# Windowed attention on one core: scores and values of each head in one matmul, own-window scores only, and another column order in the gather

## The reference, cut to what matters

```python
# 16 clouds of 512 points; 4 sorted orders; each point sees 10 neighbours per order
neigh = gather(feats, inds)                                 # per order: [B, N, 10, C], C = 32
gf = jnp.concatenate([broadcast(center), neigh - center], axis=-1)
x = stack(4 orders)[..., perm].reshape(B * N, 10, 8 * C)    # 8 heads of 32
x16 = x.astype(float16)
qh = x16.reshape(B * N, 10, nheads, 32)
scores = einsum('bihd,bjhd->bhij', qh, qh) / sqrt(32)
attn = softmax(scores, axis=-1)                             # over the 10 neighbours j
out = einsum('bhij,bjhd->bihd', attn, qh)
fused = out @ W_lin.T + b_lin                               # then conv, instance norm, leaky relu, max
```

## Time and profile before

| | before |
|---|---|
| median of 3 runs | 2311.37 us (2306.75 to 2311.55) |
| span of the profiled execution | 2306.2 us |
| DVE, PE, ACT, POOL busy in the span | 1904.0, 1865.0, 1616.7, 1007.8 us |
| SP and ACT queues' share of 16 DMA engines | 39.2% and 0.8% |

### The profile page before, as it was taken

How to read it: one execution, slowest core, us unless ns; L and a number is a source line. 1 busy time by engine, 2 the same in 40 slices (tenths; PEclk the granted TensorE clock), 3 DMA queues, 4 the chain that set the end, 5 groups by cost and what they waited for, 6 DMA issues and landing times. The chain is left out here.

```text
span 2306.2 us, 99850 instructions
## 1 busy us (share of the span) xinstructions
PE 1865.0 (81%) x37528; PEld 1286.8 (56%) x37528; DVE 1904.0 (83%) x3658; ACT 1616.7 (70%) x3249; POOL 1007.8 (44%) x995
## 2 busy tenths in 40 slices
PE   0296665888888566499999998677999999999967
PEld 0023335777777344389999997343554544454432
DVE  6798986999999599689989987783888888888865
ACT  0299985888888699689999998456555555555532
POOL 0000006999999200178888886001434444444311
PEclk9997668999999666699999999799999999999979
DMA  2103766666565167655555552212322322222210
GB/s 59 14 1 89 165 163 141 123 122 123 122 123 121 32 157 166 157 110 109 107 105 110 108 105 53 93 28 67 92 83 73 91 74 81 79 85 82 61 56 19
DMA packets 435513, 216.09 MB, mean 94 GB/s; under 512 B 301259, under 2 KB 404843, under 8 KB 435304
## 3 DMA queue, kind: packets, MB, share of 16 engines
q1 hardware_dynamic: 430120, 210.73, 39.2%
q10 hardware_dynamic: 5312, 4.31, 0.8%
HBM read 161.97 MB, written 52.96 MB: 93 GB/s over the span
## 5 line engine op out<-in xcount | busy, mean ns | idle before, releaser
L865 PE MATMUL pQ<-QM,QX 128*128 128x64 f16 (+1 forms) x5760 | 531.5, 216 | 2.1 <-issue 2.1
L863 PE MATMUL pQ<-neigh_lo,QX 128*128 128x32 f16 (+1 forms) x5760 | 519.8, 188 | 2.1 <-issue 2.1
L863 PEld LDWEIGHTS pQ<-neigh_lo,QX 128*128 128x128 f16 x5760 | 494.9, 103 | 5.4 <-issue 2.8
L865 PEld LDWEIGHTS pQ<-QM,QX 128*128 128x128 f16 x5760 | 486.9, 104 | 1.8 <-issue 1.7
L961 POOL TENSOR_TENSOR Dm<-Sc,mx 128x450 f32<-128x450 f32 x384 | 365.8, 953 | 77.8 <-DVE mx L921 77.8
L968 POOL TENSOR_TENSOR Ap<-E,R 128x450 f32<-128x450 f32 x384 | 366.0, 953 | 67.9 <-DVE R L934 57.5
L998 ACT ACTIVATE Vs<-pQ 128x480 f32<-128x480 f32 (+1 forms) x384 | 295.6, 770 | 4.7 <-PE pH L891 3.0
L930 DVE STREAM_TRANSPOSE AT<-Ap 128x480 f32<-128x480 f32 x384 | 259.3, 675 | 33.4 <-PE pH L891 10.9
L1963 POOL TENSOR_TENSOR MT<-cb,decay 128x512 f32 (+1 forms) x128 | 164.0, 1302 | 247.4 <-PEq L1731 150.6
L1011 ACT ACTIVATE E<-Dm 128x450 f32<-128x450 f32 x384 | 224.1, 584 | 60.1 <-POOL Dm L961 60.0
L921 DVE TENSOR_REDUCE mx<-Sc 128x15 f32<-128x450 f32 x384 | 224.0, 583 | 15.2 <-ACT Sc L992 15.1
(11 more groups left out here) (362 smaller groups left out, 3584.5 us busy)
## 6 DMA issues: line engine op xcount, KB each, us to landing
QM<-scratch_q SPq DMA_DIRECT2D x192, 240.0 KB, 2.7
QX<-scratch_q SPq DMA_DIRECT2D x768, 60.0 KB, 2.5
scratch_q<-QT SPq DMA_DIRECT2D x120, 360.0 KB, 4.8
Wg<-in_in_proj SPq DMA_DIRECT2D x64, 256.0 KB, 2.7
Wh<-in_in_proj SPq DMA_DIRECT2D x64, 256.0 KB, 2.8
Wo<-in_out_proj SPq DMA_DIRECT2D x64, 256.0 KB, 2.6
W_s<-in_in_proj SPq DMA_DIRECT2D x16, 256.0 KB, 2.7
CT<-scratch_c SPq DMA_DIRECT2D x192, 11.2 KB, 2.2
```

The source lines that it names most:

```text
L863: nc.tensor.matmul(pQ[:, p, u // PB, o + 32:o + BW], qx[u], W["neigh_lo"][:, 0:O], start=False, stop=True, skip_group_check=True)
L865: last = nc.tensor.matmul(pQ[:, p, u // PB, o:o + BW], qx[u], qm[u], start=False, stop=True, skip_group_check=True)
```

## The change

- Scores are made only between columns of one point. The stationary operand is one head of one sub-block (30 columns of `QX`), rows 0 to 95 hold channel times point (each row nonzero only for its own point), rows 96 to 127 the same channels for all points. The moving operand `QW` holds the K = 10 key columns (rows 0 to 95; zero below) and O weight columns (`stack`: the weights in rows 0 to 95, their rounding remainder in the last 32). So one matmul gives 10 score columns and O value columns; 60 matmuls for a tile, in four column strips. The mask, `neigh_lo` as a matmul of its own, and `Sc` are gone.
- Scores are 150 elements in a partition instead of 450. `mx`, `Dm`, `E`, `Z` work on 150. `mx` and `Dm` are both DVE's, read from `pQ`. POOL makes `RM` (`R` times a 0/1 mask `own`, 45 elements) and expands `E` to the 450 elements of `Ap`.
- Elements of one sub-block lie SW = 16 elements (32 bytes) apart in `QT`, `QX`, `QW`. In the gather DVE writes with the ten neighbour columns innermost, each 32 bytes after the last.
- SP loads for two tiles five DMAs (`QW`, three `QX` by point, one `QX` for the last 32 rows), then `CT` at once, no longer four tiles later. In layer 2, U is 6 instead of 8, and `pH` has one buffer.
- Lags: `E` 1 (2), `Z` 2 (3), transpose 3 (4), mix 4 (5), copy, square and `hmax` 5 (6).
- The start of a layer clears more and places the weights in every `QW` buffer (8 copies of 4*O*16 elements in layer 1, 6 in layer 2), over three engines.

```diff
+SW = 16
+GQ = SUBS * K
+GW = SW * K
+UT = 2
...
                     for n in range(PTS):
-                        v.tensor_tensor(flat[:, 0:W3, n * K:(n + 1) * K, :],
-                                        rows(ext, k, LEAD * K + HALF - 1 + n, (PTS * RES, W3), (1, K), (PTS, RES)),
-                                        rows(cen, k, n, (PTS * RES, W3), (0, K), (PTS, RES)),
+                        v.tensor_tensor(QT[:, k, 0:LAST, n, :, 0:SUBS].rearrange("p g j u -> p g u j"),
+                                        rows(ext, k, ahead + n, (GP, LAST), (PTS, SUBS), (1, K)),
+                                        rows(cen, k, n, (GP, LAST), (PTS, SUBS), (0, K)),
                                         ALU.subtract).then_inc(q_v, 1)
+                    v.tensor_tensor(QT[:, k, LAST, :, :, 0:REST].rearrange("p n j u -> p n u j"),
...
-    U = RV = 8
-    NQ = 8
-    ND = 4
+    U = (8, 6)[O // C - 1]
+    NP = (2, 1)[O // C - 1]
+    ND = (4, 3)[O // C - 1]
...
+                    sp.wait_ge(projected, t + UT)
+                    sp.dma_start(QW[0:96, w, :, 0:GW], rows[:, span, :]).then_inc(q_in[w], 16)
...
+                    for n in range(PTS):
+                        sp.dma_start(QX[n:96:PTS, w, :, n, :], q16[:, span, n, :]).then_inc(q_in[w], 16)
+                    sp.dma_start(QX[96:128, w, :, :, :].rearrange("p y n x -> p y (n x)"),
+                                 q16[:, span, :, :].rearrange("d y n x -> d y (n x)")).then_inc(q_in[w], 16)
...
+                    sp.wait_ge(mixed, pack(r, k + UT - 1) + 1)
+                    sp.dma_start(CT[0:2 * C, w, :], c16[:, bass.ds(r * NU + w, 1), :].rearrange("p v x -> p (v x)"))\
+                        .then_inc(c_in[w], 16)
...
                     for u in range(SUBS):
...
+                        for h in range(4):
+                            y = k % UT * 4 + h
+                            query = QX[:, w, y, :, :].rearrange("p n (j u) -> p u (n j)", u=SW)[:, u]
+                            both = QW[:, w, y, :].rearrange("p (x u) -> p u x", u=SW)[:, u]
+                            at0 = u % PB * ON
+                            last = nc.tensor.matmul(pQ[32 * h:32 * h + PTS * K, p, u // PB, at0:at0 + ON], query, both,
+                                                    start=True, stop=True)
...
+                if at(1):
+                    (t, _), p = at(1), (k - 1) % U % ND
+                    dve.wait_ge(max_ready, t + 1)
+                    dve.wait_ge(exped, t + 1)
+                    v.tensor_tensor(banks(Dm[:, p, :], K), results((k - 1) % 2)[:, :, :, 0:K],
...
+                    act.wait_ge(shifted, t + 3)
+                    act.wait_ge(mixed, pack(r, kv) + 1 + (U - RV) // SL)
+                    nc.scalar.activation(banks(Vs[:, kv % RV, :], O), results(p)[:, :, :, K:], ACT.Copy)\
+                        .then_inc(vs_ready, 1)
```

More of the change, by code:

```diff
@@ L838, in _ @@
         def _(pe):
-            pe.sem_inc(projected, NQ)
-            pe.sem_inc(mixed, RV // SL)
-            pe.wait_ge(const_in, 32)
+            pe.sem_inc(projected, U)
+            pe.sem_inc(mixed, U // SL)
+            pe.wait_ge(a_zeroed, 1)
+            none = A[:, 0:2, :].rearrange("p k x -> p (k x)").bitcast(F16)
+            for p in range(2):
+                for b in range(NB):
+                    nc.tensor.matmul(pQ[:, p, b, :], none[:, 0:128], none[:, 0:512], start=True, stop=True)
@@ new lines, in scores @@
+                    if isinstance(t, int) and t < U and k % UT == 0:
+                        pe.wait_ge(placed[w], UT)
+                    pe.wait_ge(q_in[w], r * LOADS + LOADS)
+                    pe.wait_ge(shifted, t + 1)
+                    pe.wait_ge(vs_ready, t + 1)
+                    for u in range(SUBS):
+                        for h in range(4):
+                            y = k % UT * 4 + h
[4 more added lines that the diff above has]
+                                                    start=True, stop=True)
@@ L867, in scores @@
                     last.then_inc(projected, 1)
             def mix(k, at):
-                if at(5) and (k - 5) % SL == SL - 1:
-                    t, r = at(5)
-                    k3 = (k - 5) % U
-                    q, p, ring, first = pack(r, k3), k3 // SL % 2, k3 // RV, (k3 - SL + 1) % RV
+                if at(4) and (k - 4) % SL == SL - 1:
+                    t, r = at(4)
+                    k3 = (k - 4) % U
+                    q, p, first = pack(r, k3), k3 // SL % NP, k3 - SL + 1
@@ L874, in mix @@
                     pe.wait_ge(copied, q + 1)
-                    for c in range(first // 2, (first + SL - 1) // 2 + 1):
-                        pe.wait_ge(c_in[c], (r * (U // RV) + ring) * 16 + 16)
+                    for w in range(first // UT, k3 // UT + 1):
+                        pe.wait_ge(c_in[w], r * 16 + 16)
                     strips = [(slot, half) for slot in range(SL) for half in range(O // 32)]
@@ L940, in step @@
+                if at(5) and (k - 5) % SL == SL - 1:
+                    (_, r), k5 = at(5), (k - 5) % U
+                    q, p = pack(r, k5), k5 // SL % NH
+                    dve.wait_ge(copied, q + 1 + NP)
+                    dve.wait_ge(squared, q + 1 + NH)
                     v.tensor_reduce(hmax[:, bass.ds(q * GP, GP)],
@@ L2322, in constants @@
     c["rows"] = np.stack([mid, 1 - 2.0 * mid, 1024.0 * low, 1 - 2.0 * low], 1).astype(np.float32)
-    c["maskL"] = np.array([[1024.0 * (i % 32 // K == n) * (n < PTS) for i in range(128)] for n in range(128)], np.float16)
-    c["maskR"] = np.tile(np.array([-1024.0 * (x // K != n) * (n < PTS) for n in range(128)], np.float16), (1, SUBS))
+    c["own"] = (x[:, None] // K == np.arange(PTS)[None, :]).astype(np.float32)
+    c["own"] = np.tile(c["own"], (4, 1))
     return c
```

342 lines of the change are left out of this document (154 added, 188 removed).

## The result

| | before | after |
|---|---|---|
| median | 2309.7 us (4 runs, 2306.8 to 2311.6) | 3172.9 us (4 runs, 3168.0 to 3175.1) |
| ratio | 1 | 1.3735, 95% interval 1.3714 to 1.3757 |
| span of the profiled execution | 2306.2 us | 3173.3 us |

The account below looks back on a forecast made before the run. It took ACT, closely followed by DVE, to bound the gathers, and ACT and PE to be full in attention 2. 2311 + 91 + 24 + 4 + 11 = 2441 us, stated as 2435; range 2300 to 2500.

Parts of the forecast that it names:

- Gather, +91: Both gathers: DVE's 32-byte-step writes at 1.7 ns an element, +2.84 us for each of 32 clouds, +91 us.
- the ACT row: Trace row used to price gather writes: ACT writing each element 128 bytes after the last, 1.71 ns against 0.80 contiguous.
- my upper bound of 2.1: Gather: a factor of two on DVE's rate, 2.1 ns an element, +157 us.
- Attention 2, +24: Layer 2's attention: 2.46 us a tile against 2.34 despite lower load, 192 tiles, +24 us.
- The ring through `hmax`: Attention 2: chain of waits from `hmax` through `Dm`, `E`, `Vs` and ACT's square, 4.93 us for two tiles.
- The ring of `CT`: Attention 1: `CT` waits for a mix, next pair's loads behind it; 8.0 to 8.4 us for four tiles.
- Attention 1, +4: Layer 1's attention: 2.07 us a tile against 2.05, +4 us.
- Starts, +11: Layer starts: more clearing and weight copies, +4 and +6 us, and +1 for the weights' preparation.
- The third: Rival: PE's score operands, stepping 32 bytes, take twice the time; 2511 us, chance 0.08.
- The second: Rival: full-rate gather writes and quicker rings, layer 2 -8, layer 1 -29, starts +10; 2284 us, chance 0.17.

Follow-up runs that it names:

- experiment 2: Probe in the changed kernel's gather: the three large subtractions write f16 or f32 with various output steps; f16 at 32 bytes 4.33 ns an element, f32 1.81.
- experiment 7: Changed kernel with 16-wide sub-block runs innermost in the gather, both score operands contiguous (other columns) and CT loaded four steps later: 2422.2 us.
- experiment 4: Score operands contiguous: moving alone 3054.6 us, stationary alone 3146.8, both on the changed kernel; both together with sub-blocks innermost in the gather 2563.8.
- experiment 9: CT issued by ACT instead of SyncE: on experiment 8's second kernel 2275.5 us; on its first (the second kernel here) 2457.0 us, ratio 1.0644.
- experiment 8: Later `hmax`: on the change with sub-blocks innermost and late CT 2490.4 us; on experiment 7's kernel (second) 2377.1; on the kernel before 2311.3.
- experiment 3: Gather with sub-blocks innermost: 16-wide instead of 15-wide runs, 2718.4 us; then a probe of read and output patterns, 1.01 to 1.43 ns an element.

## Why the prediction was wrong, step by step

- **Gather, +91 for +506: the step that failed most.** That DVE pays for the change's writes, becomes the bound and has no idle time was right. The price was not: "every element here begins a new piece of memory as in the ACT row" took a 4-byte row for a 2-byte write. f32 writes in such steps do cost 1.8 ns (experiment 2); f16 ones cost 4.3, outside my upper bound of 2.1. Two elements of different size are not two ends of one scale.
- **Attention 2, +24 for +176.** The ring through `hmax` was sized rightly (2.46 forecast, 2.44 measured once all else was away; experiment 7's attention 2 takes 475.0 us from first to last `E`, 24 more than before), but it was covered. The score matmul was priced 15 x (39 + 44/2.4) = 0.86 us; it takes 2.26, because both operands step by 32 bytes (0.82 with both contiguous, experiment 4). The ring of `CT` I had seen for layer 1 only. Taken off one after the other: 63 us for `CT`; the other 112 remain while PE is full (292.6 of 300 us busy in experiment 9's second kernel). They go when contiguous operands free PE and the maximum comes late: 433.6 us then from first to last `E`, for 451.4 before (experiment 8).
- **Attention 1, +4 for +170.** The mechanism, `CT`'s wait ahead of the next pair's loads, was right. The ring has 11.4 to 11.9 us, not 8.0 to 8.4: scores of two tiles 2.8 for 1.3, issues from `CT` to the fifth load 3.5 for 2.65, landing of the last load 3.4 to 3.5 for 2.6. Taken off in this order: 118 us for `CT`, 21 for `hmax`, 34 for SyncE's queue, and then it is 4 us below the kernel before. "SP's issues for a pair stay five plus `CT`: ... 3.1 us" counted the old durations: a `QX` issue with every third partition takes 0.58 us where one of the kernel before takes 0.32 (0.72 and 0.48 with the gaps in a group, as in the earlier trace rows), and most of the gaps between issues (0.1 to 0.3 us) were not in the sum.
- **Starts, +11 for +18**: the two starts grew by 4.2 and 3.1 us, near the +4 and +6; but the preparation ahead of the first gather grew by 6.4 for +1, and the 4.5 us more between attention 1 and gather 2 were not in the sum. No run took these apart.
- **Rivals.** The third (PE's operands, 0.08) was true together with the forecast's own mechanisms; I had weighed it as an alternative to them, and at twice the time where layer 2 has 2.6 times (layer 1 2.2). The second needed full-rate writes and quick rings; with the gather near its old time, contiguous operands, late centres and maximum, and one issue fewer on SyncE, the time is 2276, beside the 2284 I gave it. That is luck: the gathers cost 45 us more there, the attentions 39 and 46 less, where the rival had nothing, 29 and 8. None of these experiments with contiguous operands computes the scores. Of those that keep the computation, the best is 2457 us: no version here beats the kernel before.

What was not tried: a layout in which the moving operand is contiguous or in steps of 8 bytes and the right columns are read. Here the stationary operand is one evenly stepped run of 30 over a sub-block's three points, and the loads place whole runs of 320 bytes; a smaller step cuts those runs in pieces, and what that costs the DMA engines was not measured.

The order in which the causes are taken off decides how the 345 us of attention are shared among them; the sums by stage do not depend on it.

## What to carry to other kernels

A step between elements had a price of its own for each engine and each element size here; when no row shows the pair, widen the range to several times the nearest row, or measure it first. When no engine is full in a stage, look for the queue that only issues: add up its issues with their gaps, and ask what stands behind each wait. A wait that costs nothing under a full engine comes back when the load falls.

## What the runs showed of the hardware

- DVE writes of f16: 4.3 to 4.6 ns for each 16-byte piece begun, where that exceeds 1.04 ns an element; of f32 in steps of 16 and 32 bytes, 1.8 ns an element (experiment 2).
- Matmuls in four column strips by the step of the moving operand: 2.06 and 2.03 us for 60 x 74 columns at 32 and 16 bytes, 1.08 at 8, 0.88 at 2 (stationary steps of 32 bytes throughout). With a contiguous moving operand a stationary one in steps of 16 or 32 bytes costs some 0.4 us in 60 (0.84 and 0.88 for 0.44). The clock does not explain it: the records' mean is 270 ns where the mean granted clock of the stretch is 0.77 and where it is 1.00 (layer 1 of the changed kernel and of experiment 9's second one).
- DVE reads of f32 in steps of 3 words cost 1.38 to 1.40 ns an element in runs of 15; in steps of 1 or 2 words 1.04 (experiment 3).
- A DMA issue takes 0.32 to 0.61 us of SyncE by its shape, and mostly 0.1 to 0.3 us more pass before the next. In the changed kernel one with every third partition is the dearest, 0.58 us.
